# A ViT tower in fp32 parts: keys and queries made together, ahead of the image they belong to

## The reference

```python
h = tok(x)                      # 16x16 patches, LayerNorm, @ W + b, LayerNorm
h = h + attn(layernorm(h))      # 12 heads of 16; below
h = h + ffn(layernorm(h))       # router, attention for 29 tokens, mix for the others, MLP 192-768-192 with gelu

def attn(x):                    # causal
    q, k, v = split(x @ w_attn + b_attn, 3)        # each [128, 12 heads, 196, 16]
    q = q * 16 ** -0.5
    rel = concat([zeros_like(rel_emb[:1]), rel_emb[:196]])[:-1]
    scores = q @ k.T + q @ rel.T                   # that is q @ (k + rel).T
    y = softmax(where(causal, scores, -inf)) @ v
    return y @ w_proj + b_proj

def ffn(hs):
    normed = ln(hs); s = sigmoid(normed @ Wr + br)
    idx = the 29 tokens with the lowest s
    attn_out = softmax(q @ kk.T / sqrt(16)) @ v @ Wo + bo     # of normed
    mix_out = (normed + s * pooled) @ Wm + bm
    h = hs + where(token in idx, attn_out, mix_out)
    return h + gelu(ln(h) @ W1 + bf1) @ W2 + bf2
```

## Time and profile before

| | |
|---|---|
| median of 3 runs | 5129.2 us (5127.33 to 5132.16) |
| the profiled execution | 5130.09 us, its span 5128.4 us |
| busy: PE, PEld | 4907.1 us (96%), 4586.2 us (89%) |
| busy: DVE, ACT, POOL | 4370.3 us (85%), 3517.8 us (69%), 2906.6 us (57%) |
| granted TensorE clock, mean | 0.987 of full speed |
| one image in the loop | 38.76 us |

### The profile page before, as it was taken

How to read it: one execution, slowest core, us unless ns; L and a number is a source line. 1 busy time by engine, 2 the same in 40 slices (tenths; PEclk the granted TensorE clock), 3 DMA queues, 4 the chain that set the end, 5 groups by cost and what they waited for, 6 DMA issues and landing times.

```text
span 5128.4 us, 146889 instructions
## 1 busy us (share of the span) xinstructions
PE 4907.1 (96%) x46680; PEld 4586.2 (89%) x46680; DVE 4370.3 (85%) x13272; ACT 3517.8 (69%) x12158; POOL 2906.6 (57%) x4015
## 2 busy tenths in 40 slices
PE   3999999999999999999999999999999999999998
PEld 3899999999999999999999999999999999999997
DVE  3788888888888888888888888888888888888886
ACT  0676776776776777677677677677767767767765
POOL 2555555565565555556556556555555655655653
PEclk6999999999999999999999999999999999999998
DMA  5444444444444444434344444444444444444440
GB/s 66 57 63 60 54 66 58 57 63 59 59 60 61 60 57 64 60 54 66 57 58 63 59 60 60 61 60 57 64 60 54 65 58 58 62 59 60 60 61 16
DMA packets 338230, 301.99 MB, mean 59 GB/s; under 512 B 46796, under 2 KB 305177, under 8 KB 338201
## 3 DMA queue, kind: packets, MB, share of 16 engines
q1 hardware_dynamic: 325950, 298.98, 42.7%
q10 hardware_dynamic: 12251, 2.65, 0.4%
HBM read 205.18 MB, written 19.27 MB: 44 GB/s over the span
## 4 chain that ended last, share of the span: by engine, by line
PE 39%; issue 25%; POOL 23%; DVE 6%; POOLq 6%; ACTq 1%; DVEq 0%; DMA 0%; ACT 0%; SPq 0%
POOL p L532 8%; PE banks L741 8%; PE banks L730 7%; POOL rstd L514 5%; PE banks L674 5%; PE banks L682 5%; POOL probs_ L575 3%; POOL h L591 3%; POOLq L590 3%; PE banks L833 2%; PE banks L727 2%; POOLq L513 2%; PE banks L887 2%; DVE gparts L1216 2%; PE banks L844 2%
## 5 line engine op out<-in xcount | busy, mean ns | idle before, releaser
L1604 ACT ACTIVATE p<-banks,negmax 98x98 f32<-98x98 f32 (+1 forms) x3072 | 1138.5, 379 | 245.5 <-issue 121.7
L532 POOL TENSOR_TENSOR p<-p,rden 98x392 f32<-98x392 f32 x1152 | 959.4, 842 | 315.9 <-DVE rden L1239 309.4
L1223 DVE TENSOR_REDUCE negmax<-banks 98x2 f32<-98x392 f32 (+1 forms) x1152 | 607.8, 555 | 87.2 <-PE banks L730 83.2
L730 PE MATMUL banks<-kz,qk_parts 128*98 128x392 f32 x2304 | 632.7, 385 | 0.0
L741 PE MATMUL banks<-tokw,x_sb 128*98 128x193 f32 x3072 | 600.8, 339 | 15.4 <-POOLq L544 15.4
L1604 ACT ACTIVATION_READ_ACCUMULATOR p<-banks,negmax 98x1 f32 x3072 | 612.5, 199 | 0.0
L1669 ACT ACTIVATE f<-h,shift,rstdf 98x192 f32<-98x192 f32 x256 | 126.4, 541 | 662.3 <-DVE shift L1438 662.3
L741 PEld LDWEIGHTS banks<-tokw,x_sb 128*98 128x98 f32 x3072 | 552.7, 253 | 17.9 <-issue 15.5
L765 PE MATMUL banks<-ident,p 98*98 98x98 f32 x4608 | 523.2, 252 | 26.3 <-ACTq L1608 23.7
L547 POOL TENSOR_TENSOR gstore<-gstore 128x588 f32<-128x588 f32 x128 | 153.1, 1196 | 694.6 <-ACT gstore L1589 694.6
L682 PE MATMUL banks<-z3Ts,w_split 128*128 128x196 f32 x3840 | 515.7, 281 | 2.2 <-DVE z3Ts L1197 1.4
(11 more groups left out here) (273 smaller groups left out, 12876.2 us busy)
## 6 DMA issues: line engine op xcount, KB each, us to landing
x_sb<-in_x SPq DMA_DIRECT2D x384, 196.0 KB, 5.0
kz<-gparts SPq DMA_DIRECT2D x512, 147.0 KB, 2.9
x_sb<-in_x SPq DMA_DIRECT2D x256, 190.8 KB, 8.9
x_sb<-in_x SPq DMA_DIRECT2D x256, 185.5 KB, 10.9
x_sb<-in_x SPq DMA_DIRECT2D x128, 189.0 KB, 7.3
out<-out_row SPq DMA_DIRECT2D x128, 147.0 KB
pT<-in_L_ffn_W ACTq DMA_DIRECT2D x1, 576.0 KB
gstore<-in_L_ffn_W SPq DMA_DIRECT2D x1, 384.0 KB
```

The source lines that it names most:

```text
L532: gp.tensor_tensor(heads, heads, rden[:, g, t, s0:s0 + sn].unsqueeze(2).broadcast_to([HT, sn, w]), ALU.mult).then_inc(sem["pnorm_sb"], 1)
L730: last = mm(o, qparts[:, g, HT * t:HT * t + HT], kz[:, part, slots[0]:slots[-1] + 1, g, 0:w], start=False, stop=part == 1, skip_group_chec ...
L1223: ve.tensor_reduce(negmax[:, g, t, slots[0]:slots[-1] + 1], bank[RING[f"S{k}"]][0:HT, 0:w * len(slots)].rearrange("p (s w) -> p s w", w=w) ...
L1604: sc.activation((p1 if t else p0)[0:HT, 4 * g + s], bank[b][0:HT, w * i:w * i + w], ACT.Exp, bias=negmax[:, g, t, s:s + 1], accum_out=den[ ...
```

## The change

Keys and queries get one set of products. The weights `wkq` hold, for each group, 64 columns of keys and 64 of queries, none of them doubled; the sixth product (`add_w` x `rel_ones`) adds both biases and the relative embedding. 18 matmuls make both, into banks 2 and 3; one copy and one subtraction give `kq`. Ten DMAs then make what the score matmuls read: eight place the key parts in `kz` (16 rows each, both parts), two put the query parts into `qparts` (64 rows each). The set is made for the head's image l, at the end of the step, behind `projection`, so `place_keys` works one image further ahead and comes behind `prefetch` on SP. For that `attention_cols` (the transposes of `a_row`) moves to bank 2 and ahead of `projection`, y goes to banks 0 and 1 and gets its own buffers. The written-out orders of TensorE, VectorE and ScalarE change in many places, and on GpSimd `h2b` moves behind h1.

```diff
-    x_in=len(XROWS) * 16, out_done=16, kz_in=4 * 16,
+    x_in=len(XROWS) * 16, out_done=16, kz_in=8 * 16, q_in=2 * 16,
...
-        widths = dict(wq=NG * 128, wk=NG * 128, wv=D, fwk=D, fwv=D, fwm=D, wr=HT, w1=F)
+        widths = dict(wkq=NG * 128, wv=D, fwk=D, fwv=D, fwm=D, wr=HT, w1=F)
...
-        kz = sb("kz", [128, 2, 4, NG, T], F32R)
+        kz = sb("kz", [128, 4, 2, NG, T], F32R)
...
-        yhi, yparts = qhi, qparts
+        yhi = sb("yhi", [128, NG, T], F32R)
+        yparts = sb("yparts", [128, NG, T], F32R)
...
# SP
             def place_keys(n):
-                sp.wait_ge(sem["klo_sb"], after("klo_sb", n))
+                sp.wait_ge(sem["kqlo_sb"], after("kqlo_sb", n))
                 for s in range(4):
-                    at = slice(32 * s, 32 * s + 32)
-                    sp.dma_start(kz[at, :, s].bitcast(F32),
-                                 kparts[at].bitcast(F32)).then_inc(sem["kz_in"], 16)
+                    for r in range(2):
+                        at = 64 * r + DH * s
+                        sp.dma_start(kz[at:at + DH, s].bitcast(F32),
+                                     kq[DH * s:DH * s + DH].bitcast(F32)).then_inc(
+                                         sem["kz_in"], 16)
+                for part in range(2):
+                    sp.dma_start(qparts[64 * part:64 * part + 64].bitcast(F32),
+                                 kq[64:128, part].bitcast(F32)).then_inc(sem["q_in"], 16)
...
             with sp.Fori(0, B - 4) as j:
-                place_keys(j + 2)
                 prefetch(j + 3, j + 4)
+                place_keys(j + 3)
                 store(j)
...
# GpSimd: h2b moves from behind normalised(1) to behind h1
...
# TensorE
                 def keys():
-                    pe.wait_ge(sem["aTs_sb"], after("aTs_sb", n))
-                    group_cols(2, split["wk"], "k_mm")
-                def queries():
...
+                    if front:
+                        pe.wait_ge(sem["pT_act"], after("pT_act", n, evacuation("A4")[1]))
+                    else:
+                        pe.wait_ge(one["w_ready"], 1)
+                    pe.wait_ge(sem["aTs_sb"], after("aTs_sb", l))
+                    for g in range(NG):
+                        o, at = grouped(2)[:, g], slice(128 * g, 128 * g + 128)
+                        for i, (p, wpart) in enumerate(PAIRS):
+                            mm(o, split["wkq"][:, wpart, at], aT[:, p], start=i == 0, stop=False)
+                        last = mm(o, add_w[:, at], rel_ones[:], start=False, stop=True)
+                    last.then_inc(sem["kq_mm"], 1)
...
-                    out_of = [bank[2 + g // 2][:, (g % 2) * T:(g % 2) * T + T] for g in range(NG)]
+                    out_of = [bank[g // 2][:, (g % 2) * T:(g % 2) * T + T] for g in range(NG)]
...
# VectorE
-                def query_parts():
...
                 def keys():
-                    ve.wait_ge(sem["khi_sb"], after("khi_sb", n))
-                    ve.tensor_tensor(kparts[:, 1], grouped(2), kparts[:, 0].bitcast(F32),
-                                     ALU.subtract).then_inc(sem["klo_sb"], 1)
+                    ve.wait_ge(sem["kqhi_sb"], after("kqhi_sb", l))
+                    ve.tensor_tensor(kq[:, 1], grouped(2), kq[:, 0].bitcast(F32),
+                                     ALU.subtract).then_inc(sem["kqlo_sb"], 1)
```

More of the change, by code:

```diff
@@ L388, in build @@
                 at = 32 * s + r
-                load(bk[at:at + DH], ba[1, s])
                 load(wp[at:at + DH], wpr[s])
             load(bv[32 * s:32 * s + DH], ba[2, s])
[L392 to L395, removed]
+        for row in (64, 96):
+            for j, at in enumerate((D, 0)):
+                load(halves(brow[row:row + 1])[:, j],
+                     W["L0_attn_b_attn"][at:at + D].rearrange("(o g w) -> o g w", o=1, g=NG))
         for t, (first, r0) in enumerate(((1, 0), (0, HT - 1))):
@@ L558, in step @@
                     normalised(1)
-                if back:
-                    gp.drain()
-                    gp.tensor_tensor(h2b[:], h2[:], both(bf2), ALU.add).then_inc(sem["h2b_sb"], 1)
                 if front:
@@ L591, in step @@
                     gp.tensor_tensor(h1[:], y_row[:], both(ln2b), ALU.add).then_inc(sem["h1_sb"], 1)
+                if back:
+                    gp.drain()
+                    gp.tensor_tensor(h2b[:], h2[:], both(bf2), ALU.add).then_inc(sem["h2b_sb"], 1)
                 if head:
@@ L977, in attention_cols @@
                     pe.wait_ge(sem["a_sb"], after("a_sb", l))
-                    rows_to_cols(1, a_row, "aT_mm")
-                if front:
-                    keys()
-                    values()
+                    if front:
+                        pe.wait_ge(sem["pT_act"], after("pT_act", n, evacuation("B1")[1]))
+                    rows_to_cols(2, a_row, "aT_mm")
                 if back:
@@ L985, in step @@
                 if front:
-                    queries()
+                    values()
+                if tail:
+                    mlp_cols()
                 if back:
@@ L989, in step @@
                     keys2()
-                if tail:
-                    mlp_cols()
-                if back:
                     values2()
                     mixing_rows()
-                    gather()
                 if front:
@@ L1054, in step @@
                     projection()
+                if head:
+                    keys()
+                if tail:
+                    down(0)
                 if back:
@@ L1513, in step @@
                     gelu_parts(1)
-                if back:
-                    attn_out()
                 if head:
@@ L1519, in step @@
                     attention()
+                if head:
+                    attention_cols_lo()
+                if back:
+                    attn_out()
+                if front:
+                    residual()
                 if tail:
                     gelu_parts(2)
-                if front:
-                    residual()
                 if head:
-                    attention_cols_lo()
+                    keys()
                 if back:
@@ L1698, in step @@
                     mlp_cols_hi()
+                if front:
+                    softmax(0)
                 if back:
```

207 lines of the change are left out of this document (87 added, 120 removed).

## The result

The changed kernel takes 5159.2 us in the median (5126.1 to 5180.3 over 20 runs), the kernel before 5129.4 (5125.8 to 5132.2, 20 runs). The ratio is 1.0055, with a 95% interval of 1.004 to 1.007: slower by about half a per cent, 30 us. I had forecast 5186, 57 us more than before. The spread is itself a result: 54 us where the kernel before has 6.

A forecast was written before the change was run, and what follows sets the result against it. A chain of waits through VectorE and GpSimd, not TensorE's load, was taken to set the period. End part +1.3 and middle -0.8 us, taken as +0.45 an image over 127 steps, gave +57 us: 5186 us, range 5075 to 5240.

The forecast's parts named there:

- attn_out: VectorE operation moving from ahead of a_row, where it filled a wait, to behind it: forecast to add 0.69 us.
- the output behind z3: VectorE's output no longer fills the wait ahead of z3 but comes behind it, ahead of nTs: forecast +0.5 us.
- the end part: Stretch of the period from VectorE's a_row to score, 10.69 us before: forecast +1.3 us, bounds 0.8 and 1.6.
- the middle: Stretch from score to the next a_row, 28.07 us before: forecast -0.8 us, bounds -0.4 and -1.2.
- The new order keeps exactly this alignment, so I leave z3 at 1.29: Step for VectorE's z3: GpSimd's res still runs beside it on the shared port, so z3 stays at 1.29 us.
- if z3 no longer meets `res`: Stated sign that the forecast is wrong: VectorE's z3 no longer running beside GpSimd's res.
- it fits, so nothing: Step for h2b (1.0 us) moved on GpSimd ahead of the last rate, which waited 1.36 us: no cost.
- beside h1's statistics none does: Claim that no VectorE operation with two SBUF inputs meets the moved h2b on the shared port there.
- 0.8 us to spare: Margin between the last parts landing, 15.1 to 15.2 us after a_row, and the first scores at 16.0.
- The middle gains more: Rival: fewer collisions in GpSimd's chain outweigh the end part's loss, -0.4 us an image at the bounds, 5078 us; chance 0.27.
- TensorE as the bound: Rival: TensorE's load sets the period, so the change saves 2.1 us an image, 4861 us; chance 0.04.
- Parts so late that the image grows: Rival: ten DMAs land too late and the first scores wait, 64 us per 0.5 us beyond the margin; chance 0.07.

The follow-up runs named there:

- e4_no_queries: The kernel before the change, leaving out the 15 products of the queries' weights (three bias products stay): 5215.1 us, ratio 1.0167.
- e3_out_first: The changed kernel with VectorE's output put back ahead of z3, as before the change: 5133.7 us, ratio 1.0015 to the kernel before.
- e7_q_on_act_attn: The changed kernel with h2b back in its old place, attn_out ahead of a_row, and the queries' two DMAs issued by ScalarE: 5091.6 us, ratio 0.9932.
- e10_no_products: The changed kernel with h2b back in its old place, leaving out the shared set's 15 weight products (three bias products stay): 5117.7 us, ratio 0.9982.
- e11_no_products_attn: e7_q_on_act_attn, leaving out the shared set's 15 weight products (three bias products stay): 4997.5 us, ratio 0.9748.
- e6_q_on_act: The changed kernel with h2b back in its old place and the queries' two DMAs issued from ScalarE's queue instead of SP's: 5093.3 us, ratio 0.9933.
- e8_q_four_dmas: The changed kernel with h2b back in its old place and the query parts placed by four DMAs instead of two: 5206.5 us, ratio 1.0155.
- e9_merge_first: e7_q_on_act_attn with scatter moved ahead on TensorE, the merge ahead of the key parts on VectorE, and ScalarE's block_input later: 5139.6 us, ratio 1.0028.

## Why the prediction had the sign, but neither its cause nor its size

**Right.** The period hangs on a chain through VectorE and GpSimd, and not on TensorE's load. The saved products came back as TensorE's waits for VectorE, and `e4_no_queries` confirms it from the other side. `attn_out` (0.70 measured, 0.69 forecast), the wait for aT (0.42, 0.44), the vanished wait of the residual and the output behind z3 (0.47, 0.5) are all in the timeline. The price of an issue held, and a landing took 2.6 to 2.7 us where I had 2.9.

**The sign was luck.** I forecast "slower" because the end part would lose more (+1.3 us) than the middle gains (-0.8). It does not: an undisturbed image is 0.2 us shorter than before, and `e1_h2b_back`, the change without the moved `h2b`, is faster than the kernel before. The changed kernel is slower only by the race, which my sum had at nothing.

**The end part was mis-sized**: +1.3 forecast, +0.48 measured. The step that failed reads "The new order keeps exactly this alignment, so I leave z3 at 1.29". It did not keep it. `res` overwrites what the output reads, so with the output behind z3, `res` comes behind it as well, and from z3's start to the next start are 0.59 us instead of 1.29. The sum with this is 0.69 + 0.42 - 0.33 + 0.47 - 0.70 = +0.55. `e3_out_first` shows the long z3 coming back with the old order. I had looked at what releases `res` (the rate, h3) and not at what it must wait for before it may write. The prediction's own sign for this, "if z3 no longer meets `res`", is what happened.

**Terms that were true and did not count.** `attn_out` and the output's place each stood in the timeline as I had them, and putting either back changed no undisturbed image. The first because my layout followed VectorE's queue only: TensorE's products and ScalarE's copy behind aT end at the same point (`e7_q_on_act_attn`, `e10_no_products`, `e11_no_products_attn`). The second because what the end part gains the stretch from `zclip` to `a_row` loses, and the other way round (`e3_out_first`).

**The middle was mis-priced at one instruction.** Undisturbed it gave -0.67 of the forecast -0.8. But the step "it fits, so nothing" for the moved `h2b`, and "beside h1's statistics none does", were wrong in 65 of 125 images; what stood there in place of nothing is 0.94 us an image, and 1.26 with the clock. I had placed `h2b` beside the statistics. If `h1` wins against the cast, the GELU subtraction, which reads two SBUF operands, has slid back to where `h2b` runs. What I left out was that an operation held once is later for the next collision. Nor does it take two SBUF operands, as that sentence has it: the cast, with one, is held just as z3 was. A held operation costs about what I had read from z3 (0.65 us there; here 0.86 for the cast and 0.72 for the subtraction); its place was wrong. This is the Trainium skill's rule from page "SBUF — State Buffer", section "Who interferes with whom", at work: whoever comes first holds the pair for its whole instruction. The traces agree with it in both directions, 0.36 against 1.22 us for the same cast, and 1.01 against 1.23 for the same `h1`.

**How the two errors meet.** An undisturbed image is 0.63 us shorter than my 39.2, which z3's 0.70 covers. Over 125 images that is 79 us too much in the forecast. The lost images bring back 65 x 1.26 = 82 us in the profiled execution, fewer in the median one. That the end lay inside my range, only 27 us below the forecast, is two large errors that cancel, and so luck. The ends of the program gave 9 us where I had said nothing; I did not look into where in the setup they come from.

**The DMAs.** I had 0.8 us to spare, with the first scores at 16.0 us after `a_row` behind a `score` at 12.0. `score` came at 11.17, so the spare went with the end part's error, and the first scores wait some 0.2 us for the query parts in most images, where I had forecast no wait. In `e6_q_on_act` that wait is gone, and the period is the same.

**Rivals.** "The middle gains more" is what undisturbed images do (-0.2 us), though through the end part's z3, and what the kernel does once `h2b` is back. TensorE as the bound is refuted. Parts so late that the image grows happened only where they were forced (`e8_q_four_dmas`, `e9_merge_first`).

**What stays open.** What takes away the cast's lead of a few hundredths in the new order was not traced back to one instruction. A hint is in the runs: the cast loses images in every trace in which the query parts go out as two DMAs on SP behind the keys' eight, and none where they go out from ScalarE or in four. That the runs' spread of 54 us is the number of lost images is inferred: the three profiled executions of kernels that race twice line up with it, and the spread is gone in both orders with `h2b` back.

## What to carry to other kernels

When an instruction is moved behind another on an engine that shares a port, ask what it hits if the collision ahead of it goes the other way; a lead of 0.02 us is a coin toss, and a spread of runs that grows from 6 to 54 us is a reason to look for one. When an order is laid out by hand, list for each moved operation also the buffer that it frees, and who writes it next. And before a term is counted, look for a second chain of the same length: two remedies that each do nothing can be worth 94 us together.

## What was not expected of the hardware

Leaving out 15 products an image made the kernel before 1.7% slower. The wait that took their place, 1.85 us ahead of `score`, was followed by a stretch at 1.2 GHz in 69 of 125 images, and these took 40.00 instead of 38.78 us; the mean granted clock fell from 0.987 to 0.964. TensorE's idle time beside the chain was not free here: work that fills it can be worth keeping.
